# Attention of a fused transformer layer: the four score products of a key tile behind one wait

## The reference

```python
q, k, v = split_heads((layernorm(x) @ qkv_w.T))          # 16 heads of 8 channels
q, k = rotate(q), rotate(k)
attn = einsum('bhqd,bhkd->bhqk', q, k) * SCALE
diff = where(pos_k - pos_q > 0, 0, pos_k - pos_q)
attn = attn + diff * slopes * 8.0                         # a slope per head, no mask
out = einsum('bhqk,bhkd->bhqd', softmax(attn), v)
x = x + out.reshape(B, N, C) @ proj_w.T + proj_b
```

## Time and profile before

| | us |
|---|---|
| median of 3 runs (1000.88 to 1002.26) | 1001.54 |
| the profiled execution | 997.14 |
| its span, first to last instruction | 995.4 |
| attention, PE and ACT both in work | 324 to 796 |

### The profile page before, as it was taken

One profiled execution on the slowest core, in us unless ns is written; L12 is line 12 of the kernel. 1 busy time (PEld: TensorE's weight loads), 2 busy tenths in 40 slices (PEclk: granted clock), 3 DMA queues, 4 the chain that ended last, 5 costly groups with the idle time before them and its releaser, 6 DMA issues.

```text
span 995.4 us, 14853 instructions
## 1 busy us (share of the span) xinstructions
PE 827.1 (83%) x5629; PEld 438.3 (44%) x5629; DVE 456.9 (46%) x1198; ACT 656.6 (66%) x848; POOL 146.5 (15%) x133
## 2 busy tenths in 40 slices
PE   3288978888700999999999999999999937887888
PEld 2167756766600333333333332333232226776777
DVE  3457888888520222232212331223222237777773
ACT  1054344444010999999999999999999904554543
POOL 4423343433210000000000000000000002232221
PEclk9989999999865899999999999999999958999999
DMA  5100333322265000430022300242000021221100
GB/s 184 32 15 18 95 96 95 96 85 75 74 151 117 5 4 7 103 91 18 10 51 72 90 10 4 55 104 55 9 7 7 4 73 32 64 64 43 43 12 22
DMA packets 44940, 54.63 MB, mean 55 GB/s; under 512 B 7416, under 2 KB 30400, under 8 KB 44736
## 3 DMA queue, kind: packets, MB, share of 16 engines
q1 hardware_dynamic: 44864, 53.63, 20.4%
HBM read 33.94 MB, written 19.66 MB: 54 GB/s over the span
## 4 chain that ended last, share of the span: by engine, by line
PE 50%; issue 11%; POOL 3%; DVE 2%; DMA 1%; ACT 1%; SPq 0%; ACTq 0%; POOLq 0%; DVEq 0%
PE at_acc L1396 25%; PE at_scores L1380 22%; POOL p_hid L797 2%; PE p_ps_o L591 1%; PE p_ps_h L525 1%; DMA rope<-rden_scratch 0%; DVE p_xn L872 0%; POOL p_rstd L789 0%; ACT at_weights L1448 0%; PE p_ps_g L525 0%; ACT p_relu L719 0%; DMA q_op<-shift_rows 0%; PE p_ps_q L534 0%; PE p_ps_t L546 0%; PE p_ps_g L559 0%
## 5 line engine op out<-in xcount | busy, mean ns | idle before, releaser
L1448 ACT ACTIVATE at_weights<-at_scores 128x1024 f32<-128x1024 f32 x512 | 469.8, 1140 | 37.5 <-DVE at_scores L1433 37.5
L1396 PE MATMUL at_acc<-at_weights,v_res 128*9 128x512 f32 x2048 | 268.9, 597 | 0.8 <-ACT at_weights L1448 0.8
L1433 DVE TENSOR_TENSOR at_scores<-sdiag,at_scores 128x256 f32<-128x256 f32 x256 | 106.2, 428 | 256.7 <-PE at_scores L1380 256.2
L1380 PE MATMUL at_scores<-q_op,k_plain 29*128 29x512 f32 (+3 forms) x768 | 163.9, 440 | 37.2 <-DMA q_op<-shift_rows 35.6
L1380 PEld LDWEIGHTS at_scores<-q_op,k_plain 29*128 29x128 f32 x768 | 71.5, 183 | 235.3 <-ACT at_weights L1448 184.7
L591 PE MATMUL p_ps_o<-w_out,p_hid 128*128 128x128 f32 x1024 | 119.9, 277 | 0.1
L591 PEld LDWEIGHTS p_ps_o<-w_out,p_hid 128*128 128x128 f32 x1024 | 117.8, 194 | 0.3 <-DVE p_hid L1001 0.3
L1380 PE MATMUL at_scores<-q_op,k_full 29*128 29x512 f32 (+3 forms) x640 | 117.3, 376 | 0.0
L525 PE MATMUL p_ps_h<-p_xn_t,w_hi 128*128 128x512 f32 x256 | 93.6, 448 | 22.2 <-ACT p_relu L719 22.2
L681 ACT ACTIVATE p_coef_wide<-p_coef 128x512 f32<-128x512 f32 x64 | 35.0, 618 | 86.9 <-DVE p_coef L991 86.9
L719 ACT ACTIVATE p_relu<-p_ps_h 128x512 f32<-128x512 f32 x128 | 74.8, 591 | 26.6 <-PE p_ps_h L525 24.1
(11 more groups left out here) (148 smaller groups left out, 781.3 us busy)
## 6 DMA issues: line engine op xcount, KB each, us to landing
q_parts<-p_parts SPq DMA_DIRECT2D x24, 256.0 KB, 3.0
k_parts<-p_parts SPq DMA_DIRECT2D x24, 256.0 KB, 3.9
q_op<-q_parts SPq DMA_DIRECT2D x64, 96.0 KB
k_full<-k_parts SPq DMA_DIRECT2D x64, 96.0 KB
k_plain<-k_parts SPq DMA_DIRECT2D x64, 96.0 KB
o_scratch<-at_o_out SPq DMA_DIRECT2D x128, 18.0 KB
x_ln<-in_L_attn_x_dram SPq DMA_DIRECT2D x8, 256.0 KB, 4.3
rope<-const_rope SPq DMA_DIRECT2D x1, 2048.0 KB, 9.9
```

The costliest lines, as they stand in the source:

```text
L1380: last = nc.tensor.matmul(scores[:, u % SLOTS, i, lo:hi], k_op[at:at + ROWS, g, kt * P:(kt + 1) * P], q_op[at:at + ROWS, g, CHUNK * half + ...
L1396: last = nc.tensor.matmul(acc[BLOCK * j:BLOCK * j + VW, group % 2, :], v_res[:, c // HALVES, kt, col:col + VW], weights[:, n % PSTEPS, j, ...
L1433: v.tensor_tensor(at, sdiag[:, GH * g + 2 * pair:GH * g + 2 * pair + 2, :], at, ALU.add).then_inc(diag_added, 1)
L1448: nc.scalar.activation(weights[:, n % PSTEPS, PAIRS * pair:PAIRS * pair + 2, :], scores[:, u % SLOTS, :, :], ACT.Exp).then_inc(exps_done, 1)
```

## The change

The wait of `score(u)` for its slot goes. In its place one wait stands ahead of the two units of a key tile, for the exp that frees the later one's slot: key tile n+1 (units 2n+2 and 2n+3) is issued once exp 2n is done, then comes `weigh(n)`. Two units instead of three are made before the loop. The number of slots, the products, the adds and the exps are the same.

```diff
@@ score(u)
-                if u >= SLOTS:
-                    pe.wait_ge(exps_done, u - SLOTS + 1)
@@ the order on PE
-            for u in range(SLOTS):
+            for u in range(PAIRS):
                 score(u)
             for n in range(KT * GROUPS_ALL):
-                for u in (PAIRS * n + SLOTS, PAIRS * n + SLOTS + 1):
-                    if u < last_unit:
+                ahead = PAIRS * (n + 1)
+                if ahead < last_unit:
+                    pe.wait_ge(exps_done, max(ahead + PAIRS - SLOTS, 1))
+                    for u in range(ahead, ahead + PAIRS):
                         score(u)
                 weigh(n)
```

## The result

The changed kernel takes 1046.9 us (median of 4 runs, 1041.9 to 1048.6) beside 1001.2 for the kernel before (996.2 to 1002.3). The ratio is 1.0458, 95% interval 1.0431 to 1.0485: slower by 45.7 us, where +34 and 1036 were forecast. Put on the 1001.54 the prediction started from, the ratio gives 1047.4, just outside the range of 1025 to 1047; the profiled execution, 1041.94 us with a span of 1040.2, lies inside it. Direction and mechanism came as forecast, the size was a quarter too small: between the two profiled executions it is 44.8 us (spans of 995.4 and 1040.2) where 33.9 were reckoned. What follows is mostly about those 11 us.

What follows compares the result with a forecast made beforehand. ACT was taken as the bound. Diagonal lateness of 34.6 us, +0.5 for second waits, -0.5 for lateness already there and -0.7 for the first group gave 33.9, about +34 on 1001.54: 1036 us, range 1025 to 1047.

Steps and rivals of the forecast that it cites:

- ACT is the bound; PE's saving is worth nothing.: Attention: ACT sets the pace at 0.917 us an exp, so PE's 0.42 us less per tile gains 0.
- Tiles off the diagonal cost nothing.: The 128 key tiles off the diagonal: even exps still start in time, cost 0.
- The margin of 0.16: Off the diagonal: the even exp can start at E(2n) + 0.65 us, against a latest free start of E(2n) + 0.81.
- Each diagonal tile is late, 0.36 and 3 x 0.24, 34.6 us.: Runs of four diagonal tiles: first even exp 0.36 us late, next three 0.24 each; 1.08 in each of 32 groups.
- 0.03 until the exp (590.80 to 590.83): Diagonal tiles: 0.03 us from the end of DVE's add to the exp, part of 0.50 between product and exp.
- The first group 0.7 us better than the others: Very first group, PE at 1.2 GHz and already late: loses 0.4 us in place of 1.08, so -0.7.
- the second wait on PE +0.5: Sixteen groups beginning a batch's half with a second wait, for loads: products 0.03 us later than reckoned, +0.5 in all.
- The clock.: Rival: holes on PE drop the clock to 1.2 GHz, 0.73 us more a tile, 1050 us or above; chance 0.07.
- The range.: Whole kernel: bounds of +23 to +48 us gave 1025 to 1049, cut at the top to 1025 to 1047.
- The other price for ACT, 29 us.: ACT priced by the Trainium skill's formula, 0.95 us an exp in a row: latest start 0.85, diagonal cost 29 us.
- the 0.11: Key tile on PE: the four score products start 0.11 us behind the end of exp 2n, after the weighing.

Runs made afterwards that it cites:

- e3: The changed kernel without DVE's add on the diagonal tiles (triangular correction left out): 999.7 us, ratio 0.9992 to the kernel before.
- e4: The kernel before without DVE's add on the diagonal tiles (triangular correction left out): 999.8 us, ratio 0.9986.
- e1: The changed kernel with ACT's wait for a free weight buffer moved from the even exp to the odd exp of the tile before: 1037.2 us, ratio 1.0356.
- e10: The changed kernel run once more, unaltered, with a second profiled execution to see where the clock falls: 1044.5 us, ratio 1.0442.
- e2: The changed kernel with a third wait, for an exp long done, ahead of each even exp that has two: 1048.9 us, ratio 1.0464.
- e5: The changed kernel's order on PE, but each unit waits for its own slot as before the change: 1025.7 us, ratio 1.0243.
- e6: The changed kernel with the score products of every odd unit made twice, to fill PE's holes: 1043.8 us, ratio 1.0419.
- e9: The changed kernel with each unit waiting for its own slot and the weight-buffer wait moved off the even exp: 1021.8 us, ratio 1.0200.

## Why the prediction was nearly right in kind and wrong in size

- *ACT is the bound; PE's saving is worth nothing.* Right. e3 against e4 is the direct test: 86 us less PE work, the same time.
- *Tiles off the diagonal cost nothing.* Right: no idle time there, 132 exps in a row in e3. The margin of 0.16, or 0.10 with the second wait, held.
- *Each diagonal tile is late, 0.36 and 3 x 0.24, 34.6 us.* The chain is right in each link but one: "0.03 until the exp (590.80 to 590.83)". That row is an odd exp, which has one wait; the delayed ones are even, and from the fifth tile on they have two. With the second wait, an instruction of its own, it is 0.09. In e1, where it is away, the group loses 1.09 against the 1.08 of the sum; with it 1.33. The mis-sized term is 0.25 x 31 = 7.7 us of the 11 (four exps a group, 0.06 each). The same rise for a second wait had been read on PE in the kernel before (588.18 to 588.29) and was priced at 0.5 us there; it was not carried over to ACT.
- *The first group 0.7 us better than the others, the second wait on PE +0.5.* The first group lost 0.45 (0.4 was reckoned). The other term isn't there: groups that begin with it lose the same 1.33, as it lies behind the weighing.
- *The clock.* Its chance of 0.07 was given to a large fall. What came were short ones: 1.8 us in attention in the profiled execution, none in e10, more in e2. Of the 10.9 us between 33.9 and the profiled 44.8, the wait is 7.7, the clock 1.8, the two groups with 0.28 more 0.6, and 0.6 lie outside attention; 0.2 is not accounted for. The stages around attention move by more than that from profile to profile without any change in their code (199.9 us behind the last exp before, 201.7 after, 204.3 in e10; the first exp at 324.5, 323.4 and 328.5), so that a difference of 2 or 3 us in the time of one execution says nothing about attention.
- *The range.* Its upper end came from bounds of which none was this wait; its cut from 1049 to 1047 was a matter of trust, not of rows. That the profiled execution fell inside is partly luck: it is the fastest of the four.
- *The other price for ACT, 29 us.* It keeps the 0.11 that was reckoned with a pace of 0.917; with its own 0.95 that is 0.08 and the sum 28. It was further off than the rows' 34.6.

## What to carry to other kernels

Where one engine is full and keeps its pace, work taken off another gains nothing, and what a change may lose is read as a chain: release, product, add, start of the instruction, against the latest start that costs nothing. Merging two waits into the later of them takes from the first consumer the head start it had. Off the diagonal the chain, 0.65 us as reckoned and 0.71 with the second wait, still fitted into 0.81 and nothing was lost; on it the chain of 1.11 to 1.22 as measured did not, and that was paid in every round. When a link of the chain is priced from a row, the instruction in that row must have as many waits as the one it stands for, and a wait that is always satisfied can be moved to an instruction that has time: in e1 that alone gave back 0.24 us a group.

## What the hardware showed that was not expected

- An exp with two waits starts 0.06 us later behind the add than one with one (0.094 in place of 0.034), although the other wait was satisfied long before. The compiled program puts one of the two into an instruction of its own, and here it is the one for the add, that is met last. A third wait goes into the same instruction and adds 0.02. Ahead of an exp that ACT is not yet ready for (the odd one in e1) none of it costs anything.
- An exp's reported start tells little when ACT is full: queued exps show up to 1.29 us, but their ends lie 0.917 apart. Idle time plus 0.10 gives the true lateness here.
- In the changed kernel one exp at the head of a run, in the seventh and again in the 23rd group, is 0.28 us later than the others of its kind, in both profiles of it (idle time 0.59 in place of 0.31). The same two groups show it in e2, e5 and e6, where the even exp has the separate wait instruction too, and not in e1 and e9, where it has none. The delay lies between that instruction and the exp, 0.34 us in place of 0.06. No run looked into its cause.
